# First FFN1 tile: five decoding operations move from behind column chunk 2 to behind column chunk 0

## The reference

```python
x = x + 0.5 * ffn(layernorm(x))        # FFN1
x = x + attention(layernorm(x))
x = x + 0.5 * ffn(layernorm(x))        # FFN2, same weights

def ffn(x):                            # H = 512, I = 1408
    gate_up = x @ dequant_fp4(gate_up_packed, gate_up_scales).T
    gate, up = gate_up[..., :I], gate_up[..., I:]
    y = (silu(gate) * up) @ dequant_fp4(down_packed, down_scales).T
    return y / sqrt(mean(y * y) + 1e-6)
```

## Time and profile before

| | |
|---|---|
| median of 3 runs | 2580.82 us (2577.58 to 2581.5) |
| the profiled execution's own time | 2581.73 us, its span 2579.8 us |
| mean granted clock of TensorE | 0.995 of full speed |
| PE busy | 2480.4 us, 96% of the span |
| DVE busy | 1811.5 us, 70% |
| POOL busy | 1532.8 us, 59% |
| ACT busy | 1460.7 us, 57% |

### The profile page before, as it was taken

How to read it: one execution, slowest core, us unless ns; L and a number is a source line. 1 busy time by engine, 2 the same in 40 slices (tenths; PEclk the granted TensorE clock), 3 DMA queues, 4 the chain that set the end, 5 groups by cost and what they waited for, 6 DMA issues and landing times.

```text
span 2579.8 us, 39633 instructions
## 1 busy us (share of the span) xinstructions
PE 2480.4 (96%) x14559; PEld 1099.3 (43%) x14559; DVE 1811.5 (70%) x3100; ACT 1460.7 (57%) x2829; POOL 1532.8 (59%) x1537
## 2 busy tenths in 40 slices
PE   5899999999999999999999999999999999999998
PEld 3444444444443444433344434444333444444443
DVE  7866666678659594948586695858475866666666
ACT  6666666665225656565632255565665466666664
POOL 3466666764325767676342266676774467766775
PEclk9999999999999999999999999999999999999999
DMA  2012211121122020200140221020004301111101
GB/s 67 17 42 77 95 42 50 50 98 50 50 59 61 6 51 10 64 6 3 60 155 33 70 50 44 14 50 25 3 4 154 116 17 50 50 50 50 50 33 49
DMA packets 78017, 130.57 MB, mean 51 GB/s; under 512 B 19552, under 2 KB 24699, under 8 KB 77695
## 3 DMA queue, kind: packets, MB, share of 16 engines
q1 hardware_dynamic: 77822, 128.05, 16.1%
HBM read 68.23 MB, written 31.46 MB: 39 GB/s over the span
## 4 chain that ended last, share of the span: by engine, by line
PE 79%; DVE 7%; ACT 4%; issue 2%; SPq 1%; POOL 1%; DMA 0%; DVEq 0%; ACTq 0%; POOLq 0%
PE pp L97 60%; PE ps L97 18%; ACT sb L103 4%; DVE sb L112 4%; DVE sb L118 1%; SPq L139 1%; POOL sb L106 1%; DVE sb L109 1%; PE ps L100 1%; DVE sb L106 1%; DMA sb<-sb 0%; PE pp L100 0%; DVE sb L115 0%; DVE sb L124 0%; DVE sb L127 0%
## 5 line engine op out<-in xcount | busy, mean ns | idle before, releaser
L97 PE MATMUL pp<-sb,sb 128*128 128x512 f16 (+8 forms) x11230 | 2068.5, 420 | 32.4 <-DVE sb L112 12.8
L106 POOL TENSOR_TENSOR sb<-sb,sb 128x512 f32<-128x512 f32 (+7 forms) x1353 | 1491.1, 1128 | 1019.4 <-ACT sb L103 349.3
L97 PEld LDWEIGHTS pp<-sb,sb 128*128 128x128 f16 (+3 forms) x11230 | 799.5, 102 | 1068.2 <-issue 213.9
L97 PE MATMUL ps<-sb,sb 128*128 128x512 f16 (+8 forms) x2786 | 723.7, 348 | 35.1 <-DVE sb L112 21.6
L103 ACT ACTIVATE sb<-pp 128x512 f32<-128x512 f32 (+6 forms) x1035 | 521.2, 560 | 331.9 <-PE pp L97 317.1
L118 DVE TENSOR_REDUCE sb<-pp 128x1 f32<-128x512 f32 (+3 forms) x704 | 440.3, 665 | 150.2 <-PE pp L97 149.9
L103 ACT ACTIVATE sb<-sb 128x512 f16<-128x512 f32 (+4 forms) x513 | 326.2, 650 | 376.1 <-DVE sb L112 327.7
L112 DVE SCALAR_TENSOR_TENSOR sb<-pp,sb,sb 128x512 f32<-128x512 f32 x447 | 324.0, 745 | 137.8 <-PE pp L97 118.3
L112 DVE SCALAR_TENSOR_TENSOR sb<-ps,sb,sb 128x512 f32<-128x512 f32 x437 | 316.0, 745 | 136.6 <-PE ps L97 113.9
L97 PEld LDWEIGHTS ps<-sb,sb 128*128 128x128 f16 (+3 forms) x2786 | 249.9, 98 | 351.0 <-DVE sb L112 46.4
L103 ACT ACTIVATE sb<-ps 128x512 f32<-128x512 f32 (+5 forms) x473 | 262.8, 567 | 153.5 <-PE ps L97 123.6
(11 more groups left out here) (29 smaller groups left out, 376.8 us busy)
## 6 DMA issues: line engine op xcount, KB each, us to landing
sb<-sb SPq DMA_DIRECT2D x144, 128.0 KB, 2.4
sb<-L_attn_X SPq DMA_DIRECT2D x64, 256.0 KB, 3.6
sb<-xa SPq DMA_DIRECT2D x64, 256.0 KB, 4.2
sb<-xc SPq DMA_DIRECT2D x64, 256.0 KB, 3.4
xa<-sb SPq DMA_DIRECT2D x32, 256.0 KB, 2.0
xc<-sb SPq DMA_DIRECT2D x32, 256.0 KB, 4.3
out<-sb SPq DMA_DIRECT2D x32, 256.0 KB, 2.0
sb<-sb SPq DMA_DIRECT2D x48, 96.0 KB, 2.1
```

The costliest lines, as they stand in the source:

```text
L97: return self.e.matmul(*a, **k) if self.e else self
L106: return self.e.tensor_tensor(*a, **k) if self.e else self
```

## The change

In the first tile, for row chunks 0 to 7, the plan's decode events of five operations stand behind column chunks 0 and 1 in place of 1 and 2; the last two ors stay behind column chunk 3. Since the twelve operations keep their order, what happens in DVE's queue is that the first five move from column chunk 1 to column chunk 0, and the second five from column chunk 2 to column chunk 1. No instruction is added or taken away on any engine, and no DMA moves.

```diff
                     if first and c == 0 and i == 0:
                         yield "decode", 2, 99
-                    if first and c and i + 3 < IC:
+                    if first and c != 2 and i + 3 < IC:
                         yield "decode", i + 3, 5 if c < 3 else 99
```

## The result

| | before | changed |
|---|---|---|
| median | 2579.69 us (2577.58 to 2581.5, 6 runs) | 2598.52 us (2594.49 to 2605.53, 6 runs) |
| ratio of the runs | | 1.0076, 95% interval 1.0065 to 1.0086 |
| span of the profiled execution | 2579.8 us | 2599.7 us |
| mean granted clock of TensorE | 0.995 | 0.989 |

The change costs 18.8 us. Two stretches of the changed kernel (columns as in the earlier trace rows) show where. The first answers to 30.42 to 117.00 us of before and ends 23 us later; its clock is 0.77 where it was 0.94. The second, which leaves out the last 20 us of the span, answers to the stretch in which PE sets the time, and PE is as busy in it as before: 97.7% against 97.5%.

A forecast was written before the change was run, and what follows sets the result against it. DVE's evacuations, with PE following, were taken to bound the first tile's decoding, PE the rest from about 130 us. Queue order +9.3 and clock falls +6.4 gave +15.7: 2596.5 us, range 2587 to 2605.

The forecast's parts named there:

- The two mechanisms: First tile: longer rounds from DVE's queue order, +9.3 us, and more falls of PE's granted clock, +6.4 us.
- The chunk 1 evacuation loses its cover: DVE's queue: this evacuation, hidden in the wait for POOL's widening, would come after the first five, 0.66 us a round.
- The first five stay at their place behind POOL: DVE's first five still wait for POOL's widening and run beside its four operations, ending 5.41 us into the stretch; price 0.
- B to A 8.45 us: From PE's first transpositions of a round to DVE's down-weight subtraction: 8.45 us where it was 6.73.
- PE's two stands: PE idle before the column chunk 2 transpositions and before the down-weight subtraction: 2.2 and 1.5 us, where it stood 1.88.
- A to B is set by PE's twelve, 2.74 us: From DVE's down-weight subtraction to PE's next first transpositions: twelve matmuls, not DVE's 2.24, close the round; 2.74 against 3.11.
- The sum of the order, +9.3: First-tile round changes from DVE's queue order, without the clock: +1.35 in a usual round, +9.3 us in all.
- The clock, 4 falls at 1.6 us, +6.4: PE's longer standing drops its granted clock over the twelve matmuls, four times in rounds 1 to 7: +6.4 us.
- falls in nearly every round: Rival: PE's clock falls in nearly every first-tile round or stays low through a whole round; +20 to +30 us, chance 0.08.
- one fall in each round: Skill's rule on PE cycling through PSUM banks, applied to seven rounds: 9.3 + 11.2 = 20.5 us.
- DVE's queue alone: Rival: PE's twelve matmuls don't close the round, only the chunk 1 evacuation loses its cover; +5.1 us, no falls, chance 0.07.
- The relief from POOL: Rival: POOL's four operations come later than DVE's first five, which take 1.06 not 2.90 us; -3.6 us, chance 0.03.

The follow-up runs named there:

- the first five alone: Kernel before with only the first five decode operations moved, column chunk 1 to 0; second five stay behind chunk 2: 2587.08 us, +6.5, ratio 1.0025.
- the filled versions: Matmuls of zeros where PE stands: changed kernel with 9 and 6, 2586.95 us (its profile is the filled one); kernel before with 8, 2579.73 us.
- the other direction: Kernel before with decoding moved later, five operations behind column chunk 2 and seven behind 3: 2579.8 us, ratio 0.9997; all twelve behind 3: 2583.25 us, ratio 1.0015.

## Why the prediction was right

The prediction said +15.7 us, 2587 to 2605; it is +18.8. The two mechanisms are the ones it named, and the experiments separate them. Their sizes were off in opposite directions, so part of the nearness is luck: with the measured order (7.2) and the forecast clock the sum is 13.6, with the measured clock (12.5) and the forecast order 21.8. Either would still have lain in the range.

- *The chunk 1 evacuation loses its cover, +0.66 a round.* Shown by the first five alone: +0.84 a round (10.68 against 9.84), 0.66 of it this and 0.18 the wait between two evacuations on one accumulator, which was not foreseen.
- *The first five stay at their place behind POOL, with masks at full price.* Right: they wait for POOL and the masks take 2.69 or 2.70 us in each of row chunks 1 to 7.
- *B to A 8.45 us.* 8.41 in the changed kernel (61.59 to 70.00), 8.24 at full clock. PE's two stands in it were put at 2.2 and 1.5 us and are 1.92 and 1.30.
- *A to B is set by PE's twelve, 2.74 us.* 2.74 at full clock (66.04 to 68.78), to the hundredth. That B has no idle time before it was right as well.
- *The sum of the order, +9.3.* Too high: 7.2 between the filled versions (6.4 against the kernel before, which has a little low clock of its own). In the filled profile the three rounds from row chunk 2 to 5 cost 1.14 each, not 1.35; the round after row chunk 0 costs 0.46 where 1.31 was reckoned, since in that profile the clock does not start low; A of row chunk 0 comes 0.3 us later and not 1.06; and row chunk 8 gives back 1.74, not 0.87. The last is a step of the sum that was missed. Four small norm operations that took 2.76 us beside POOL's work (108.12 to 110.88 in the profile before) now come just ahead of it (these rows are of the changed kernel):

```profile
129.72 0.57 DVE L109 TENSOR_SCALAR sb<-sb 128x4 f32<-128x4 f32 x3
130.32 0.16 DVE L106 TENSOR_TENSOR sb<-sb 128x4 f32<-128x4 f32 x1
```

- *The clock, 4 falls at 1.6 us, +6.4.* Too low, and the larger error. The term was mis-sized in both factors. In the profile PE's matmuls behind A run at low clock, at least in part, in each of row chunks 1 to 7: seven falls in place of four. And A to B is 5.23 us (70.00 to 75.23) against 2.74, so a fall costs 2.5 in row chunks 2 to 5, where it covers all of the twelve; it costs 2.2 and 2.0 in row chunks 6 and 7 and 0.4 in row chunk 1, which has six matmuls there. The 1.7 of the prediction was read from a fall of before that covered only part of the twelve. The seven add up to 14.6 us in this execution, which ran 3.1 over the median; from the medians the clock's share is 2598.52 - 2579.69 less 6.4, some 12.5 us. The case "falls in nearly every round" had a chance of 0.08 and is what the profiled execution shows; its time, +20 to +30, would have missed by a little, because the order was reckoned too dear. The three fastest runs (+14.8 to +15.7) had less low clock than that, so for them four falls may have been nearer; no profile of them was kept.
- The rule of the Trainium skill ("TensorE: Matmul & The Clock Gate", section "A second HAM failure mode: psum-queue depth-cycling") says that a kernel which cycles through PSUM banks can swing between the two clock levels; it names no number of falls. The trace of the changed kernel agrees, with a clock of 0.77 over the decoding stretch. Taken as one fall in each round, the prediction's sum was 20.5 us, 1.7 above the measured time where its own forecast was 3.1 below.
- *Other rivals.* DVE's queue alone is out: B follows PE. The relief from POOL did not come, because the first five wait for POOL and so cannot get out of its way; in the other direction, where they could, the masks did fall to 0.88 us. The ors and the product slow down beside POOL as well, 2.87 us against 1.22. The Trainium skill ("GPSIMD Engine Reference", section "Key points") says that DVE instructions with two SBUF inputs contend with GpSimd, and the trace agrees.

What stays open is why the clock low settles so evenly: three successive rounds of 13.64, 13.65 and 13.66 us. The rows of the result show the clock going down and up in step with them, full until just ahead of A, half until after B, then full again. Whether the round takes its length from that swing, or the swing from the round, no run tested. The six runs of the changed kernel lie between 2594.5 and 2605.5, wider than any other version. Their mean clock goes with the time (0.992, 0.991 and 0.993 at 2594.5, 2595.4 and 2595.1 us; 0.989 and twice 0.988 at 2601.6, 2605.1 and 2605.5), so the spread goes with the low clock too.

## What to carry to other kernels

Ask of every wait what work is lying in it before moving an operation: an evacuation that fills an engine's wait is free until it is put behind that wait. A queue change on one engine can be worth more through TensorE's clock than through the queue: here 7 us of order brought 12 us of clock, with two stands of PE, and little work between, just ahead of the twelve matmuls that close the round. And a "hidden" operation has the slack of the engine beside it, not its own length: PE's twelve had 0.3 us to spare, and 1.06 was asked of them.

## What was not expected of the hardware

- Work that computes nothing can make a kernel faster: 15 matmuls of zeros in each round took the changed kernel from 2598.5 to 2587.0 us. Only the stationary operand is zeros, and the clock held (1.00 from 60 to 80 us, against 0.78).
- DVE's operations on two SBUF operands slow down beside POOL as the masks do: three of them 2.87 us in place of 1.22; and small ones of 4 columns too, 2.76 us for four in place of 0.76.
- Two evacuations in a row that add to the same accumulator, the second waiting for the first's signal, cost 0.18 us of waiting (88.26 to 88.44 in the first five alone); where other operations stand between them it doesn't appear.
